# Layer 0's values as column strips, layer 1's keys inside the combine loop, its fourth feature folded into weights, its routing in halves

## The reference, cut to what matters

```python
x = x + attn0(ln(x), ctx)    # ctx [8, 64, 128]; 16 heads of 8; one k and one v head of 8 shared by all
x = x + soft_moe(ln(x))      # 16 experts, 64 slots each
x = x + attn1(ln(x), ctx)
x = x + moe1(ln(x))          # 64 experts of width 88, top 8; and a shared MLP of width 176
...                          # attention, top-2 MoE, attention, quantised conv FFN

def attn0(x, ctx):
    q = (x @ Wq) in 16 heads, * 8 ** -0.5;  k, v = split(ctx @ Wkv)
    return (softmax(q k^T) @ v over all heads) @ Wo
def attn1(hc, hq):           # hc = ln(x): [8, 256, 128], hq = ctx
    Sim = (hc @ w1)[:, :, None] + (hq @ w2)[:, None, :] + (hc * w3) @ hq^T + b
    hq_hat = softmax(Sim, 2) @ hq
    hc_bar = softmax(max(Sim, 2), 1) @ hc          # one row of 128 per batch
    return [hc, hq_hat, hc * hq_hat, hc * hc_bar] @ W_qv + b_qv
def moe1(x):
    s = sigmoid(x @ gate_w.T); c = s + bias        # 64 scores, 8 groups of 8
    # groups are rated by the sum of their two largest c, the best 4 groups stay,
    # of these the 8 largest c are picked; weights are their s, normalised, * 2.5
    return sum over picked experts of weight * mlp_e(x) + shared_mlp(x)
```

## Time and profile before

| | us |
|---|---|
| median of three runs | 994.78 (996.98, 991.86, 994.78) |
| the profiled execution | 999.47 |
| its span | 997.7 |

### The profile page before, as it was taken

How to read it: one execution, slowest core, us unless ns; L and a number is a source line. 1 busy time by engine, 2 the same in 40 slices (tenths; PEclk the granted TensorE clock), 3 DMA queues, 4 the chain that set the end, 5 groups by cost and what they waited for, 6 DMA issues and landing times. The chain is left out here.

```text
span 997.7 us, 15949 instructions
## 1 busy us (share of the span) xinstructions
PE 930.0 (93%) x4685; PEld 722.5 (72%) x4685; DVE 709.9 (71%) x1657; ACT 522.4 (52%) x1005; POOL 572.8 (57%) x541
## 2 busy tenths in 40 slices
PE   7899899799987899999999999999999889999796
PEld 5678666466686656888888888888887776677664
DVE  5765677899744688866666666666667878886865
ACT  3444566445562255666666666666664334453354
POOL 5511344577713035877777777777776628884500
PEclk9998999999998889999999999999999789999998
DMA  6000000222100000000000000000002000000001
GB/s 189 2 1 1 1 1 1 75 63 63 42 1 27 1 9 3 28 25 24 24 24 24 24 24 24 24 24 25 26 9 106 0 1 1 1 1 1 1 11 33
DMA packets 27112, 23.99 MB, mean 24 GB/s; under 512 B 3419, under 2 KB 23987, under 8 KB 26803
## 3 DMA queue, kind: packets, MB, share of 16 engines
q1 hardware_dynamic: 27059, 23.34, 7.8%
HBM read 22.28 MB, written 1.05 MB: 23 GB/s over the span
## 5 line engine op out<-in xcount | busy, mean ns | idle before, releaser
L1779 PE MATMUL psum<-xw 128*128 128x512 f32 x1248 | 322.7, 394 | 3.9 <-DVE xw L1416 2.6
L666 POOL TENSOR_TENSOR hh<-arena,hh 128x512 fp32r<-128x512 f32 x176 | 227.9, 1295 | 82.2 <-ACT hh L815 80.8
L1779 PEld LDWEIGHTS psum<-xw 128*128 128x128 f32 x1248 | 232.3, 188 | 56.0 <-issue 7.2
L1615 DVE TENSOR_TENSOR psum<-psum,arena 128x512 f32<-128x512 f32 x176 | 123.0, 699 | 101.0 <-PE psum L1779 94.7
L1058 ACT ACTIVATE arena<-psum 128x512 f32<-128x512 f32 x176 | 105.3, 598 | 120.2 <-PE psum L1779 120.1
L815 ACT ACTIVATE hh<-arena 128x512 fp32r<-128x512 f32 x228 | 142.4, 626 | 47.5 <-DVE arena L1714 45.2
L1779 PE MATMUL psum<-hh,wdn 128*128 128x512 f32 x528 | 148.4, 390 | 0.2 <-POOL hh L666 0.2
L1620 DVE TENSOR_TENSOR arena<-psum,arena 128x512 f32<-128x512 f32 x176 | 121.6, 691 | 7.6 <-DVE psum L1615 1.7
L1779 PE MATMUL psum<-arena 128*128 128x18 f32 (+7 forms) x776 | 111.5, 322 | 10.3 <-ACT arena L815 6.5
L1779 PEld LDWEIGHTS psum<-hh,wdn 128*128 128x128 f32 x528 | 98.9, 188 | 21.1 <-POOL hh L666 0.5
L1779 PEld LDWEIGHTS psum<-arena 128*128 128x128 f32 (+3 forms) x776 | 90.1, 196 | 19.9 <-ACT arena L815 9.3
(11 more groups left out here) (292 smaller groups left out, 1534.5 us busy)
## 6 DMA issues: line engine op xcount, KB each, us to landing
egu<-in_w SPq DMA_DIRECT2D x44, 128.0 KB, 2.0
egu<-in_egu SPq DMA_DIRECT2D x16, 256.0 KB, 2.6
edn<-in_w SPq DMA_DIRECT2D x44, 64.0 KB, 1.8
edn<-in_edn SPq DMA_DIRECT2D x16, 128.0 KB, 2.1
arena<-in_w SPq DMA_DIRECT2D x1, 1536.0 KB, 6.8
X<-in_x SPq DMA_DIRECT2D x4, 256.0 KB, 4.2
arena<-in_conv SPq DMA_DIRECT2D x1, 1024.0 KB, 8.9
out<-X SPq DMA_DIRECT2D x4, 256.0 KB, 2.3
```

The source lines that it names most:

```text
L666: pool.tensor_tensor(hh[:, s % 4, 1, :], h1[:, s % 2, :], hh[:, s % 4, 0, :].bitcast(F32), ALU.subtract).then_inc(hh_lo, 1)
L1615: dve.tensor_tensor(bank(2 + k), bank(2 + k), sil[:, k, :], ALU.mult).then_inc(prod_done, 1)
L1779: return pe.matmul(dst, lhsT=lhsT, rhs=rhs, start=start, stop=stop)
```

## The change

Four parts.
*Values.* `vaug` becomes `vstrip` (v in 32 columns, one set for each parity of the tile of weights) and `ostrip` (ones in the same places). `values` makes y transposed, in four strips of 32 rows: 16 products for y and 16 for the denominators, each spread over 128 columns. VectorE's reciprocal has 128 columns and its product is y transposed, so `outputs_T0` and `output_rows` go.
*Keys.* Inside the combine loop at t = 7 to 13 stand the transposes and logits of the groups 0 and 1, the constants `dw2T` and the sums; `cw` is made at t = 1. The logits are two products of 64 rows each.
*Fourth feature.* hc_bar is made transposed at once, one column per batch. For each batch VectorE folds it into the weights: `wfold` = W_qv[fourth] * hc_bar + W_qv[first]. A tile then has three products. The first two (`features`) stand two tiles ahead of the third. Layer 3's first transposes and router logits stand in the loop.
*Expert layer.* ScalarE applies the norm of layer 3, with a bias that GpSimd makes; the sigmoid follows each half; `routing` is called for each half; the first half's weights are transposed, split and spread among the shared products, with the copies on ScalarE alone; `last_rows` does the second half after the second gate product.

```diff
 # TensorE, values(u)
-                for j in range(H0 // 2):
-                    w = 2 * (HD + 1)
-                    last = mm(psum[:, 6, w * j:w * j + w], simET[:, u % 2, P * j:P * j + P],
-                              vaug[:, b].rearrange("p h k -> p (h k)"))
+                for k, w in enumerate((vstrip[:, b], ostrip)):
+                    for par in range(2):
+                        for j in range(4):
+                            own, at = slice(32 * j, 32 * j + 32), P * (2 * j + par)
+                            last = mm(psum[own, 6, P * k:P * k + P], w[:, par, :], simET[:, u % 2, at:at + P], par == 0, par == 1)
...
 # VectorE, layer 0's turn
-                    av = psum[:, 6, 0:H0 * (HD + 1)].rearrange("p (h k) -> p h k", k=HD + 1)
-                    then(dve.reciprocal(rden0[:, u % 2, :], av[:, :, HD]))
-                    if u >= 2:
-                        dve.wait_ge(yT_ready, u - 1)
-                    dve.tensor_tensor(y0[:, u % 2], av[:, :, 0:HD], wide(rden0[:, u % 2, :].unsqueeze(2), H0, HD), ALU.mult)\
-                        .then_inc(y_ready, 1)
+                    then(dve.reciprocal(rden0, psum[:, 6, P:2 * P]))
+                    dve.tensor_tensor(y0T[:, u % 2, :], psum[:, 6, 0:P], rden0, ALU.mult).then_inc(y_ready, 1)
...
 # TensorE, combine loop
+                if t == 7:
+                    ln_transpose(2, 0)
+                    pe.wait_ge(w_rest, 16 * (len(REST) + 1))
+                    for q in range(B // 2):
+                        last = mm(psum[:, 0, q:q + 1], ctxT[:, P * q:P * q + P], cols[:, COL["w_sim2"]:COL["w_sim2"] + 1])
+                    last.then_inc(simT_mm, 1)
+                if t == 9:
+                    sim_rows(0)
+                if t == 10:
+                    pe.wait_ge(wsum_done, 1)
+                    mm(psum[:, 1, 0:2], ones[:, :], wsum).then_inc(wsum_mm, 1)
+                if t == 11:
+                    ln_transpose(2, 1)
+                if t == 13:
+                    sim_rows(1)
...
+            ln_transpose(2, 2)
+            pe.wait_ge(x_done, NT + 14)
+            sim_T(0)
+            sim_T(1)
+            sim_rows(2)
+            ln_transpose(2, 3)
+            sim_T(2)
+            sim_rows(3)
+            sim_T(3)
...
 # VectorE, feature loop
-                if g == 1:
-                    dve.wait_ge(hc_sb, 2)
-                    for b in range(B):
-                        last = dve.tensor_scalar(xcT[:, N * b:N * b + N], xnT[:, N * b:N * b + N], hcT[:, b:b + 1], None, ALU.mult)
+                dve.scalar_tensor_tensor(wfold[:, b, :], wqv[:, 3, :], hcT[:, b:b + 1], wqv[:, 0, :], ALU.mult, ALU.add).then_inc(wfold_done, 1)
...
             for t in range(NT):
                 dve.wait_ge(qv_ready, t + 1)
                 dve.tensor_tensor(X[:, t, :], psum[:, 3 + t % 3, 0:D], X[:, t, :], ALU.add).then_inc(x_done, 1)
+                if t % 2 == 0 and t // 2 + 2 < B:
+                    folded(t // 2 + 2)
                 norm_behind(3, t)
...
 # TensorE, feature loop
-                pe.wait_ge(xc_done, t // 8 + 1)
                 if t >= 3:
                     pe.wait_ge(x_done, 2 * NT + t - 2)
-                for k, feat in enumerate((xnT, hqT, xhT, xcT)):
-                    last = mm(psum[:, 3 + t % 3, 0:D], feat[:, P * t:P * t + P], wqv[:, k, :], k == 0, k == 3)
-                last.then_inc(qv_ready, 1)
+                mm(psum[:, 3 + t % 3, 0:D], hqT[:, P * t:P * t + P], wqv[:, 1, :], True, False)
+                mm(psum[:, 3 + t % 3, 0:D], xhT[:, P * t:P * t + P], wqv[:, 2, :], False, False)
+            features(0)
+            features(1)
+            for t in range(NT):
+                if t + 2 < NT:
+                    features(t + 2)
+                pe.wait_ge(wfold_done, t // TB + 1)
+                mm(psum[:, 3 + t % 3, 0:D], xnT[:, P * t:P * t + P], wfold[:, t // TB, :], False, True).then_inc(qv_ready, 1)
+                if t == 11:
+                    ln_transpose(3, 0)
+                if t == 13:
+                    router_logits(0)
...
 # ScalarE, expert layer
+                act.wait_ge(ln_rstd, NG * 3 + g + 1)
+                for t in range(4 * g, 4 * g + 4):
+                    last = act.activation(xn[:, t, :], X[:, t, :], ACT.Identity, scale=rstd[:, t:t + 1], bias=veps[:, t:t + 1])
+                last.then_inc(ln_xn, 1)
...
             for g in range(NG):
+                shared_out(g)
+                if g >= 1:
+                    for e in ((0, 1), (2,), (3,))[g - 1]:
+                        for q in range(2):
+                            weight_row(e, q, 2 * e + q)
...
 # TensorE, expert layer
+            ln_transpose(3, 1)
+            pe.wait_ge(x_done, 3 * NT)
+            shared_gate_up(0)
+            router_logits(1)
+            pe.wait_ge(xh_lo, E0 + 1)
+            shared_gate_up(1)
+            ln_transpose(3, 2)
+            router_logits(2)
+            ln_transpose(3, 3)
+            router_logits(3)
+            for m in range(2, 2 * NG):
+                if m == 6:
+                    pe.wait_ge(rl_sig, 2)
+                    weights_T(0)
+                    weights_T(1)
                 shared_gate_up(m)
+            pe.wait_ge(xh_lo, E0 + NG)
+            shared_down(0)
+            shared_down(1)
+            weight_rows(0, 0)
+            weight_rows(1, 0)
+            shared_down(2)
+            weight_rows(2, 0)
+            shared_down(3)
+            weight_rows(3, 0)
+            pe.wait_ge(rb_sb[0], 2 * RG)
             chunk_group1(0, True)
```

More of the change, by code:

```diff
@@ L602, in _ @@
             then(pool.tensor_tensor(rowmask[:, :], headmask[:, 0:H0 // 2], headmask[:, H0 // 2:H0], ALU.add))
[L604 to L609, removed]
+            pool.memset(vstrip, 0.0)
+            then(pool.memset(ostrip, 0.0))
+            for par in range(2):
+                for r in range(2):
+                    at = 16 * par + HD * r
+                    last = pool.memset(ostrip[C * r:C * r + C, par, at:at + HD], 1.0)
+            last.then_inc(consts, 1)
+            pool.wait_ge(consts, 2)
+            pool.tensor_copy(identb[:, :], ident[:, :])
             def ln_power(L, g):
@@ L999, in _ @@
             act.wait_ge(simT_sb, 1)
[L1000 to L1007, removed]
-                    last = act.activation(simT[own, q, :], psum[own, q, N * r:N * r + N], ACT.Identity, bias=dw2T[own, q:q + 1])
-                last.then_inc(simT_sb, 1)
+            sim_rows(0)
+            ln_evac_group(2, 1)
+            sim_rows(1)
+            ln_evac_group(2, 2)
+            sim_rows(2)
+            ln_evac_group(2, 3)
+            sim_rows(3)
             for hf in range(2):
@@ L1594, in routing @@
-                then(dve.reciprocal(rsum1[:, 1, :], rsum1[:, 0, :]))
-                for q in range(NG):
-                    r = slice(4 * q, 4 * q + 4)
-                    dve.tensor_tensor(rw[:, r, 0, :], t3[:, r, :], wide(rsum1[:, 1, r].unsqueeze(2), 4, E1), ALU.mult).then_inc(rw_done, 1)
-            norm_low(3, 2)
-            norm_low(3, 3)
-            routing()
-            for q in range(NG):
+                then(dve.scalar_tensor_tensor(t3[:, r, :], t2[:, r, :], -3.0e38, sc1[:, r, :], ALU.is_equal, ALU.mult))
@@ L1611, in hidden1 @@
+            routing(0)
+            routing(1)
+            weights_low(2)
+            weights_low(3)
+            for e in range(RG):
+                dve.wait_ge(rb_mm, 2 * RG + 2 * e + 2)
+                dve.tensor_copy(rwb[:, e, 1536:2048], bank(row_bank(e, 3))).then_inc(rb_sb[1], 1)
+            dve.wait_ge(rb_sb[0], 3 * RG)
             def hidden1(n, s):
@@ L1904, in _ @@
                         last.then_inc(se_tp, 1)
-                if grouped and t >= 3:
-                    outputs_T0(t - 3)
                 if grouped:
@@ L2124, in _ @@
             pe.wait_ge(ctx_in, 16)
-            for b in range(B // 2):
+            for b in range(B):
                 attended(b)
@@ L2137, in _, with router_logits, features @@
-            pe.wait_ge(aT_sb, 2)
-            for t in range(NT):
+            def router_logits(g):
+                pe.wait_ge(ln_xnT, 3 * NG + g + 1)
+                for t in range(4 * g, 4 * g + 4):
+                    last = mm(psum[:, t // 8, E1 * (t % 8):E1 * (t % 8) + E1], xnT[:, P * t:P * t + P], gw1[:, :])
+                if g % 2:
+                    last.then_inc(rl_mm, 1)
+            def features(t):
                 pe.wait_ge(xh_done, t // 8 * 2 + 2)
-                pe.wait_ge(xc_done, t // 8 + 1)
```

328 lines of the change are left out of this document (162 added, 166 removed).

## The result

The changed kernel takes 1000.04 us (median of 8 runs, 998.86 to 1011.35), the kernel before 994.36 (8 runs). The ratio is 1.0086 with a 95% interval of [1.0058, 1.0114]: slower by 5.8 to 11.3 us (5.7 between the medians), where I had forecast 996 and "no change" as the likeliest case. The time lies in the range, near my slower rival at 1002 to 1003, but not by that rival's mechanism: the strips are faster than I took them to be.

A forecast was written before the change was run, and what follows sets the result against it. No engine bounds the whole kernel; unchanged expert loops fill most of the span. Terms -5.0 - 4.0 + 4.6 + 6.7 = +2.3 on 994.8 gave 997.1, less 1 for the clock: 996 us, 8-in-10 range 983 to 1009.

The forecast's parts named there:

- slower rival: Layer 0's values: strips at 1.86 us plus 0.2 gain 1 us or nothing, 1002 us; slower case near 1003, chance 0.26.
- four signs: Turns of 3.9 to 4.0 us, feature additions 1.36 apart, last subtraction 4 us earlier, silu 0 over 12 us behind.
- Value strips: Layer 0's attention: plain turns go from 4.20 to 3.95 us, bound passing to VectorE; -5.0 us, between -6 and +1.
- term of 1.5 us for the 32 passes: TensorE's turn in layer 0: 1.3 us for the strips plus 0.1 on each side for entering and leaving the tile shape.
- no overlap: Layer 0's values: column tiles don't overlap, strips take 3.5 us and a turn 6.0; 1026 us, chance 0.07.
- issue bounds them: Layer 0's values: rate of issue, 0.058 us a pass, makes 1.86 us for 32; 1002 us, slower case's chance 0.26.
- Keys early: Layer 1's attention: 3.6 us of work moves into the combine loop, softmax input ends earlier; -4.0 us, between -3 and -5.
- may hold one up by a microsecond: Behind the combine loop: GpSimd's bias addition (4.8 us) overlaps the last VectorE operations, so -4.7 us was taken as -4.0.
- Fourth feature: Feature loop: becomes one serial chain of 1.36 us a round, 20.6 us against 14.6, with 1.4 won at the start; +4.6 us.
- won at the start: Feature loop's start: without the transpose of h's average the first addition comes 1.4 us earlier.
- Routing in halves: Layer 1's expert entry: late silu 0 and row copies outweigh the halved broadcast; +6.7 us, between 0 and +10.
- silu 0 13.1 us behind the addition: Expert entry: queue order on ScalarE and TensorE sets the first silu 13.1 us behind the last addition, 10.7 before.

The follow-up runs named there:

- values_before: The changed kernel with layer 0's values, transpose of y and reciprocal as they were before the change; 1007.98 us, ratio 1.0168 to the kernel before.
- features_behind: The changed kernel with features(t + 2) placed behind tile t's last product instead of ahead of it; 992.43 us, ratio 1.0002 to the kernel before.
- best4: best3 with the 32 passes that average h made 128 columns wide instead of 1; 981.1 us, ratio 0.9883 to the kernel before.
- norm_on_vector: The changed kernel with layer 3's norm applied by VectorE again, as before; 998.1 us, ratio 1.0062 to the kernel before.
- keys_before: The changed kernel with the keys part undone, its work again behind the combine loop; 1009.47 us, ratio 1.0166 to the kernel before.
- max_copy_late: The changed kernel with VectorE's two small copies of the row maxima moved behind both subtractions; 1010.3 us, ratio 1.0164 to the kernel before.
- best3: The changed kernel with features behind the last product, the old expert entry and 27 unread filler products on TensorE; 983.1 us, ratio 0.9904 to the kernel before.
- experts_before: The changed kernel with the whole fourth part, layer 1's expert entry, undone; 990.57 us, ratio 0.9992 to the kernel before.
- rows_shared: The changed kernel with the second of each pair of first-half row copies on VectorE instead of ScalarE; 1004.64 us, ratio 1.0112 to the kernel before.

## Why the prediction was right or wrong

Of the four signs that I had named for "right", three came: plain turns without idle time on VectorE (3.79 us, a little under 3.9), feature additions 1.38 us apart, and silu 0 over 12 us behind. The last subtraction, to come 4 us earlier behind the combine loop's start, came 2.1 earlier.

*Value strips*, forecast -5.0: -6.8 at full clock, give or take a microsecond or two. Direction and mechanism held, and VectorE is the bound as forecast. A plain turn is 3.79 us and not 3.95 because VectorE's instructions follow each other more closely than I had added up: 1.14 from subtraction to reciprocal (I took 1.26) and 0.19 from addition to the next maximum (0.28). Mis-sized was also the term of 1.5 us for the 32 passes, 1.01; it is off the path in plain turns. The bound of issue that I had taken from eight bf16 passes, 0.058 each, does not hold for them: 32 passes in 1.01 us are 0.032 each. The rivals "no overlap" and "issue bounds them" are out. I had taken 1 us for the half clock in the median; *values_before* lies 8 us above the changed kernel, where the strips' own gain is 5 to 7, so it is rather 1 to 3.

*Keys early*, -4.0: -2.1 (+3.5 and -5.6). The added work in the loop was right to 0.1 us. The step that failed is "may hold one up by a microsecond": the copy was held up for four, and moving it away gave 1.85 us of tail back.

*Fourth feature*, +4.6: +6.6. The serial chain was right (1.36 and 1.38 a tile; +6.0 in the loop), and its cause is shown by *features_behind*. The 1.4 us "won at the start" were not won. I counted the average of h as "the same 32 passes" and they are, in time; but now they stream one column each, the clock fell inside them, and the products behind took twice as long. I also left out that two further products now stand ahead of the first tile's last one. *best4* shows the first for the best kernel and *features_behind* the second (0.8 us); in the changed kernel itself wide passes were not tried.

*Routing in halves*, +6.7: +8.7. Shared down with rows was forecast +4.5 and is +4.6, the halved broadcast -3.0 and is -2.9. Mis-sized is the rest, forecast at +5.2: the shared products end 30.1 us behind the end of the last addition and not 28.3, so it is +7.0. Most of that is "silu 0 13.1 us behind the addition", which came at 14.7, counted from the same end. ScalarE's apply is 1.64 us for a group and not 1.15, twice on the path, and the last logits ran at half clock (1.97 instead of 1.0). And two products ran at half clock behind the idle time, not one. *norm_on_vector* shows the share of ScalarE's apply, 2.7 us at silu 0.

The sum of the terms at full clock was +2.3; their measured values are -6.8 - 2.1 + 6.6 + 8.7 = +6.4, with the rest near nothing, and 5.7 between the medians. So the miss of 4 us is three terms missed by 2 each against one that was better by 1.8; that the total came this near, and inside the range, is in part luck. What I had wrong in kind is the clock: I charged it as a fee per stage. *keys_before* and *max_copy_late* show that its state is carried from one stage into the next: an edit that shortens its own stage by 1.9 us cost 8 to 10 in the whole.

## What to carry to other kernels

Where a loop has a product whose operand is late, put the early products of later tiles behind it in TensorE's queue when they wait for a bank: two lines here were worth some 8 us. Price an edit near a change of TensorE's clock by the granted clock of the stages behind it as well, and look at it in the profile of every variant, since a shorter stage can make the whole slower. A gain in work that is spread into another engine's idle time is real only when the wait that it makes in an ordered queue is counted: ScalarE and TensorE paid more for the early rows than the late ones had cost.

## What the runs showed of the hardware

- TensorE's clock fell to half while the trace has the engine 100% busy, in 32 passes of one column each (316.6 to 320.9 us in best3; in all eight profiles that entered such passes at full clock), and not when the same passes had 128 columns (*best4*).
- The same serial loop ran at full clock when entered at full clock (20.3 to 21.0 us, in the changed kernel, *values_before*, *norm_on_vector*, *experts_before* and *rows_shared*) and at half clock nearly to its end when entered at half (27.9 us, in *keys_before* and *max_copy_late*).
- 32 passes of 128 columns on strips of 32 output partitions took 1.01 us, 16 full ones of 18 columns 1.70.
- A VectorE copy of 128x8 took 4.44 us beside GpSimd's addition of 128x2048, and a 128x128 operation with two SBUF inputs 1.36 us instead of 0.28 beside an addition of 88x512 on GpSimd that took 1.27 (L1598 of the changed kernel, at 365.95).
